# Edge groups of 512 instead of 1024, their keys spread by TensorE, in a graph network's count tables

## The chip, the cores and the metric

The kernel is one program on one core of a Trainium2 chip. The metric is the device time of one execution in microseconds (us).

## The reference

There are four layers on 3125 nodes with 256 features and 53,125 edges, sorted by their target. Each one adds to x what it makes of a layer-normalized x: three graph convolutions (a mean over each node's neighbours, two weight matrices, batch norm), slice attention, a hypergraph convolution, and a mixture of eight experts. For the change only the first graph step counts:

```python
agg = segment_sum(h[src], dst, num_segments=N)
deg = segment_sum(ones, dst, num_segments=N)
out = (agg / maximum(deg, 1)) @ Wl + bl + h @ Wr
```

All graph layers use the same edges.

## The kernel before

**Tables.** The kernel turns the edge list into a dense table of counts in DRAM, edges from node to node, in 16-bit floats. The table has five blocks (NB = 5) of 640 target nodes (BC), and a block has 128 x 16000 counts, 4.1 MB. Aggregation is then a matmul of the node features with the table's chunks. There are two tables, `at_counts` and `odd_counts`, so that scatters into the one can run while those into the other land. Later DVE adds each odd chunk to the even one (`sum_tables`, L1210), ACT writes the sum back (L780), and PE aggregates (L1860 for the degrees, L1868 for the features, L1886 for the products with the weights). The last block is done in two halves (L1221, L1922, L1931, L1950).

**Clearing.** ACT issues DMAs that write zeros into the tables (L704, one per table and block) from `zeros16`, which lies in a buffer that the first layer's output overwrites later. The first two are issued at the start. Then ACT issues nine small loads of vectors (L712) and two of weights (L713, L714), and then, for b = 1 to 4, waits until both tables' block b-1 is cleared and issues both clears of block b. Only after this loop come ACT's square root for the layer norm (`ln_sqrt(1)`, L722) and the copies for the first layer, which wait until everything is cleared.

**Keys.** Each edge has a key, its address in the table. The keys stand as `ekeyT` (104 rows of 512, one row per partition) and as `ekey` (416 columns of 128, made by PE's transposes). Scatters add, but a key that stands twice in one scatter, or in two scatters in flight, would be lost. So DVE compares each column of 128 with all the keys of its group: `edges_of`, one SCALAR_TENSOR_TENSOR with an accumulator per column (L1104), and three small operations per group (L1109 to L1111). They give one of the equal edges the count, and send the others to spare cells. A group is GQ = 8 columns, 1024 edges; there are NG = 52 groups. Its keys must be on all 128 partitions: SP stores `ekeyT` to DRAM (`key_rows`, L434) and loads each group back, broadcast, into one of LOOK = 4 buffers (L437, L443).

**Scatters.** POOL issues one indirect DMA per column (L598), eight for an even group into `at_counts`, eight for the next into `odd_counts`. Before each group it waits for the group's indices (`idx_ready`) and for all scatters of the group before the last, which went to the same table. Before the first group it waits until the blocks that the first eight groups touch are cleared, and before the ninth until all are.

**Order on DVE.** Each engine runs its program in order. DVE compares two turns of LOOK groups (8 groups); then it takes the layer norm's statistics of x, waits for ACT's square root, works out the release counts (`block_releases`), and goes into a loop of five, each with the normalized rows of five tiles, one turn of groups, and the low halves of those rows. The rest of the turns follow, and then the sums of the tables.

**Order on SP.** It starts loading table chunks only when all groups are compared, since chunks and `ekey` share the buffer `ring`. It loads a block when POOL's scatters of that block have landed (`released`).

```python
            ln_sqrt(1)
            wait(w0_in, 16 * 11)
            wait(zeroed, 2 * 16 * (NB + 1))
```

Of the kernel before, what the change touches and what calls it, by code (L numbers as in the profile page):

```python
# [4 lines left out]
P = 128  # L5
# [7 lines left out]
NB = T // BT  # L13
# [6 lines left out]
EC = -(-EDGES // P)  # L20
GQ = 8
GE = GQ * P
NG = EC // GQ
RW = 512
ER = EC * P // RW
RQ = RW // P
LOOK = 4
FIRST_GROUPS = 8
GROUP = GQ * 16
AROW = T * BC  # L30
# [66 lines left out]
def build(nc, x, src, dst, w, out):  # L97
    ctx = ExitStack()
    with ctx:
# [19 lines left out]
        ad = ad_flat.rearrange("(b p r) a -> p b (r a)", b=NB, p=P)  # L119
        key_rows = dram("key_rows", (EC * P,), fp32)  # L120
        xn_rows = dram("xn_rows", (T * P, F), fp32)
# [4 lines left out]
        ring = sb("ring", [P, 8192])  # L126
# [35 lines left out]
        def halves(d):  # L162
# [21 lines left out]
        release = harena[0:1, 11320:11320 + 4 * NR].bitcast(i32).rearrange("p (a b) -> p a b", a=4)  # L184
        row_block, first_block = harena[0:ER, 11313:11314], harena[0:1, 11314:11315]
        ekey = ring[:, 0:EC]
        espare = ring[:, EC:2 * EC]
        eweight = ring[:, 832:832 + 2 * GE - P]
        weight_ps = ps[:, 4:8, :].rearrange("p k c -> p (k c)")[:, 0:2 * GE - P]
        krow = ring[:, 2752:2752 + LOOK * GE].rearrange("p (a c) -> p a c", a=LOOK)  # L190
        ejunk = [late[:, q * GE // 2:(q + 1) * GE // 2].bitcast(fp16) for q in range(6)] + [
            ring[:, 6848 + q * GE // 2:6848 + (q + 1) * GE // 2].bitcast(fp16) for q in range(GQ - 6)]
        ecount = ring[:, 7872:7872 + 4 * GQ].rearrange("p (a c) -> p a c", a=4)
# [49 lines left out]
        for k in range(2):  # L243
# [63 lines left out]

        consts_ready, filled, edges_in, x_in, zero_ready, zeroed = map(sem, (
            "consts_ready", "filled", "edges_in", "x_in", "zero_ready", "zeroed"))
        fold_in, fold_pe, fold_dve = map(sem, ("fold_in", "fold_pe", "fold_dve"))  # L310
        keys_dve, key_stored = map(sem, ("keys_dve", "key_stored"))
        piece_in = [sem(f"keys_or_last_piece_in{s}") for s in range(LOOK)]
        compared, idx_ready, even_added, odd_added, tables_summed = map(sem, ("compared", "idx_ready", "even_groups_added", "odd_groups_added", "tables_summed"))
# [49 lines left out]
        def last_in(q):  # L363
            if q < LOOK:
                return piece_in[q], 16 * (NG // LOOK + 1)
            return odd_in[0], 16 * (-(-(NB * NB) // 2) + 1)
# [54 lines left out]
        def _(sp):  # L421
# [10 lines left out]
            sp.dma_start(bsl_row, w["L0_ffn_b_slice"].rearrange("(a g) -> a g", a=1)).then_inc(fold_in, 16)  # L432
            sp.wait_ge(keys_dve, 1)
            sp.dma_start(key_rows.rearrange("(p c) -> p c", c=RW), ekeyT).then_inc(key_stored, 16)  # L434
            sp.wait_ge(key_stored, 16)
            for s in range(LOOK):
                sp.dma_start(krow[:, s, :], key_rows[s * GE:(s + 1) * GE].partition_broadcast(P)).then_inc(piece_in[s], 16)  # L437
            sp.dma_start(xrows[:, 0:T - 1, :], x[0:(T - 1) * P, :].rearrange("(t p) d -> p t d", p=P)).then_inc(x_in, 16)
            sp.dma_start(xrows[0:TAIL, T - 1, :], x[(T - 1) * P:N, :]).then_inc(x_in, 16)
            with sp.Fori(0, NG // LOOK - 1) as i:  # L440
                for s in range(LOOK):
                    sp.wait_ge(compared, LOOK * i + (s + 1))
                    sp.dma_start(krow[:, s, :], key_rows[bass.ds(i * (LOOK * GE) + (s + LOOK) * GE, GE)].partition_broadcast(P)).then_inc(piece_in[s], 16)  # L443
            sp.wait_ge(idx_ready, NG)
# [115 lines left out]
        def _(pool):  # L560
# [31 lines left out]
            def add_group(g, table, added):  # L592
# [4 lines left out]
                for c in range(g * GQ, (g + 1) * GQ):  # L597
                    nc.gpsimd.indirect_dma_start(  # L598
                        out=table, out_offset=bass.IndirectOffsetOnAxis(ap=eidx[:, c:c + 1], axis=0),
                        in_=evalue[:, c:c + 1], in_offset=None, compute_op=ALU.add).then_inc(added, 16)  # L600

            pool.wait_ge(idx_ready, 1)
            cleared = pool.value_load(release[:, 3, 0:1], min_val=64, max_val=64 + 32 * (NB - 1))
            pool.nop(nofuse=True)
            pool.wait_ge(zeroed, cleared)
            pool.nop(nofuse=True)
            for g in range(0, NG, 2):
                if g == FIRST_GROUPS:
                    pool.wait_ge(zeroed, 32 * (NB + 1))
                add_group(g, at_flat, even_added)  # L610
                add_group(g + 1, odd_flat, odd_added)

# [78 lines left out]
        def _(act):  # L691
            def wait(s, value):
                act.wait_ge(s, value)
                if not isinstance(value, int):
                    act.nop(nofuse=True)
# [6 lines left out]

            def clear(table, b):
                act.dma_start(table[:, b, :].rearrange("p (k c) -> p k c", c=ZW), zeros16[:, 0:ZW].unsqueeze(1).to_broadcast([P, AROW // ZW, ZW])).then_inc(zeroed, 16)  # L704

            for flat in (at_flat, odd_flat):
                act.dma_start(flat[ASIZE:ASIZE + GE * SPREAD, :].rearrange("(p n) a -> p (n a)", p=P), zeros16[:, 0:GE * SPREAD // P]).then_inc(zeroed, 16)
            clear(at, 0)
            clear(odd, 0)
            for l in range(3):  # L710
# [49 lines left out]
            wait(w0_in, 16 * 11)  # L760
            wait(zeroed, 2 * 16 * (NB + 1))
            wait(fold_dve, 6)
# [193 lines left out]
        def _(dve):  # L956
# [9 lines left out]
            def step(ins):  # L966

                o.mark(ins)
                o.settle()
# [7 lines left out]
            for k in range(2, NB):  # L977
# [8 lines left out]
            dve.wait_ge(fold_pe, 1)  # L986
            step(V.tensor_reduce(first_block, ps[0:1, 1, 0:2 * FIRST_GROUPS], AX.X, ALU.max))
            step(V.tensor_scalar(release[:, 3, 0:1], first_block, 32.0, 64.0, ALU.mult, ALU.add))
# [109 lines left out]
            def edges_of(i, ahead, groups=range(LOOK)):  # L1098

                for s in groups:  # L1100
                    dve.wait_ge(piece_in[s], i * 16 + (16 * ahead + 16))
                    g = i * (LOOK * GQ) + (ahead * LOOK + s) * GQ
                    for q in range(GQ):
                        ins = V.scalar_tensor_tensor(out=ejunk[q], in0=krow[:, s, :], scalar=ekey[:, bass.ds(g + q, 1)], in1=weight_ps[:, GE - P - q * P:2 * GE - P - q * P],  # L1104
                                                     op0=ALU.is_equal, op1=ALU.mult, accum_out=ecount[:, s, q:q + 1])
# [642 lines left out]
        def _(pe):  # L1748
# [87 lines left out]
            def nothing_between(q):  # L1836
                pass
# [455 lines left out]
```

## Time and profile before

| | us |
|---|---|
| median of 3 runs (2973.86 to 2995.41) | 2974.38 |
| the profiled execution | 2977.06 |
| its span | 2975.3 |
| busy PE, DVE, POOL | 2255.9, 1308.3, 889.9 |

The span is the time from the first to the last instruction in the trace, and what is left to the execution's own time lies around it. All row times count from the span's start.

### The profile page before, as it was taken

Reading aid. Unit: us, or ns where it says so; the run is one execution under the profiler, and the core shown is the slowest. Engines: PE = TensorE matmul, PEld = TensorE weight load, DVE = VectorE, ACT = ScalarE, POOL = GpSimd, SP = SyncE. Lnnn points to the kernel's source line nnn. Section 1 sums busy time; section 2 is a strip of 40 time slices with the busy share of each in tenths; the row PEclk is TensorE's granted clock in tenths of the full one; section 3 lists DMA queues with packets and bytes.
Section 4 is the critical chain, followed back from the end, with each engine's and each line's share of the span. In section 5 each row is a group of like instructions: output and inputs, shape, how many; then the busy total and the mean of one; then the engine's idle time right before and its main releaser. Section 6 shows DMA issues by size and latency. Waiting matters only on the chain.

```text
span 2975.3 us, 39530 instructions
## 1 busy us (share of the span) xinstructions
PE 2255.9 (76%) x14177; PEld 1771.6 (60%) x14177; DVE 1308.3 (44%) x2804; ACT 375.5 (13%) x789; POOL 889.9 (30%) x637
## 2 busy tenths in 40 slices
PE   1033200048989999999996878999999995899997
PEld 1022100035667776777773457888888884788886
DVE  7899999955341011111116855012311667111111
ACT  0011000000005000004102212001110000222222
POOL 4888888886830000000002410000000001333332
PEclk9976555569999999999997979999999986999999
DMA  9943333368770999960351000444344434567766
GB/s 346 329 80 50 44 48 50 50 215 282 188 227 0 234 194 261 248 184 0 100 188 50 0 1 1 144 144 132 123 142 143 143 104 130 163 190 210 211 194 176
DMA packets 298822, 425.26 MB, mean 143 GB/s; under 512 B 165858, under 2 KB 235513, under 8 KB 298655
## 3 DMA queue, kind: packets, MB, share of 16 engines
q1 hardware_dynamic: 116575, 295.72, 30.7%
q10 hardware_dynamic: 109760, 108.33, 13.3%
q0 software_dynamic: 72400, 20.04, 7.8%
q8 instruction: 55, 0.90, 0.1%
q14 instruction: 32, 0.26, 0.0%
HBM read 306.57 MB, written 100.17 MB: 137 GB/s over the span
## 4 chain that ended last, share of the span: by engine, by line
PE 64%; DVE 16%; issue 7%; DMA 4%; POOL 3%; ACT 2%; ACTq 2%; DVEq 1%; SPq 0%
PE ps L1868 16%; PE ps L2166 8%; PE ps L2167 8%; PE ps L2248 7%; PE ps L2239 7%; DVE late L1104 5%; PE ps L1800 4%; PE ps L1886 4%; DMA odd_counts<-tarena 3%; DVE ring L1104 3%; POOL at_counts L598 2%; PE ps L1999 2%; PE ps L2100 2%; PE ps L2123 2%; DMA xrows<-odd_counts 1%
## 5 line engine op out<-in xcount | busy, mean ns | idle before, releaser
L2166 PE MATMUL ps<-harena,ring 128*128 128x257 f16 x2500 | 558.1, 275 | 3.1 <-DVE harena L1521 1.4
L2167 PE MATMUL ps<-harena,ring 128*128 128x256 f16 x2500 | 557.7, 273 | 0.0
L1868 PE MATMUL ps<-ring,harena 128*128 128x320 f16 x3800 | 512.4, 297 | 1.4 <-ACT tarena L755 0.8
L1868 PEld LDWEIGHTS ps<-ring,harena 128*128 128x128 f16 x3800 | 371.8, 98 | 138.5 <-issue 3.1
L1104 DVE SCALAR_TENSOR_TENSOR late<-ring,ps 128x1024 f16<-128x1024 f32 x312 | 379.0, 1276 | 12.9 <-DMA ring<-key_rows 10.7
L598 POOL DMA_INDIRECT at_counts<-harena x208 | 330.2, 1588 | 111.7 <-issue 108.8
L598 POOL DMA_INDIRECT odd_counts<-harena x208 | 331.2, 1592 | 63.9 <-issue 63.0
L2166 PEld LDWEIGHTS ps<-harena,ring 128*128 128x128 f16 x2500 | 243.2, 97 | 42.1 <-DVE harena L1521 4.5
L2167 PEld LDWEIGHTS ps<-harena,ring 128*128 128x128 f16 x2500 | 243.4, 97 | 33.3
L652 POOL IOTA harena<- 1x32 int32 x1 | 0.2, 183 | 736.4 <-DVE xrows L1590 736.4
L1892 PE MATMUL ps<-ident,sc 128*1 128x128 f32 x4 | 1.0, 333 | 281.3 <-DVE sc L1050 281.3
L2248 PE MATMUL ps<-ring,harena 128*128 128x256 f32 x896 | 201.7, 382 | 10.4 <-ACT harena L948 8.9
L2239 PE MATMUL ps<-harena,ring 128*128 128x256 f32 (+1 forms) x1024 | 201.5, 355 | 1.2 <-DVE harena L1721 1.2
L2248 PEld LDWEIGHTS ps<-ring,harena 128*128 128x128 f32 x896 | 167.6, 190 | 39.2 <-issue 17.7
L2239 PEld LDWEIGHTS ps<-harena,ring 128*128 128x128 f32 x1024 | 177.0, 192 | 22.3 <-issue 1.6
L1185 DVE SCALAR_TENSOR_TENSOR feat<-ps,sc,late 128x640 f32<-128x640 f32 x30 | 26.5, 884 | 348.5 <-PE ps L1868 348.5
L623 POOL DMA_DIRECT2D wl<-L_ffn_W_out x1 | 0.7, 712 | 586.8 <-DVE feat L1185 586.8
L681 POOL DMA_INDIRECT x_sum<-harena x56 | 88.8, 1586 | 268.0 <-DVE harena L1731 237.3
L1892 PEld LDWEIGHTS ps<-ident,sc 128*1 128x1 f32 x4 | 0.2, 81 | 282.0 <-issue 282.0
L948 ACT ACTIVATE harena<-ps,harena 128x256 f32<-128x256 f32 (+1 forms) x256 | 114.4, 447 | 342.4 <-PE ps L2239 337.9
L1886 PE MATMUL ps<-feat,wl 128*128 128x320 f32 x448 | 125.5, 441 | 16.5 <-DVE feat L1185 15.5
L1800 PE MATMUL ps<-feat,wr 128*128 128x320 f32 (+1 forms) x480 | 130.1, 428 | 0.0
(395 smaller groups left out, 2556.0 us busy)
## 6 DMA issues: line engine op xcount, KB each, us to landing
ring<-at_counts SPq DMA_DIRECT2D x145, 800.0 KB, 4.4
ring<-L_ffn_W SPq DMA_DIRECT2D x64, 1024.0 KB, 5.6
ring<-ad_counts SPq DMA_DIRECT2D x50, 800.0 KB, 4.2
ring<-key_rows SPq DMA_DIRECT2D x52, 512.0 KB, 3.7
at_counts<-tarena ACTq DMA_DIRECT2D x5, 4000.0 KB, 15.3
odd_counts<-tarena ACTq DMA_DIRECT2D x5, 4000.0 KB, 27.7
at_counts<-ring ACTq DMA_DIRECT2D x25, 800.0 KB, 7.0
ad_counts<-xrows ACTq DMA_DIRECT2D x25, 800.0 KB, 7.6
```

Source lines behind the costliest of these rows:

```text
L598: nc.gpsimd.indirect_dma_start(out=table, out_offset=bass.IndirectOffsetOnAxis(ap=eidx[:, c:c + 1], axis=0), in_=evalue[:, c:c + 1], in_of ...
L681: nc.gpsimd.indirect_dma_start(out=x_sum, out_offset=bass.IndirectOffsetOnAxis(ap=to_row[:, j:j + 1], axis=0), in_=yrow[c % 2][:, i, :], i ...
L948: nc.scalar.activation(hT[s][:, k, 0:n], ps[:, k % 4, 0:n], ACT.Gelu, bias=evc[s][:, k:k + 1]).then_inc(e_gelu, 1)
L1104: ins = V.scalar_tensor_tensor(out=ejunk[q], in0=krow[:, s, :], scalar=ekey[:, bass.ds(g + q, 1)], in1=weight_ps[:, GE - P - q * P:2 * GE ...
L1800: ins = M(ps[:, 4 + n % 4, 0:c], weights[:, d, fo * P:(fo + 1) * P], feat[:, d, h * HB:h * HB + c], start=(d == 0), stop=(d == 3))
L1868: ins = M(ps[:, 2 * f + h, 0:c], part[:, t, (2 * k + f) * P:(2 * k + f + 1) * P], chunk[q][:, s, h * HB:h * HB + c], start=(t == 0 and par ...
L1886: ins = M(ps[:, k + h, 0:HB], wl2[:, d, fo * P:(fo + 1) * P], feat[:, d, h * HB:(h + 1) * HB], start=(d == 0), stop=(d == nfi - 1))
L1999: return M(ps[:, i % 4, 0:F], feat[:, d, i * P:(i + 1) * P], wl3[:, d, :], start=(d == 0), stop=(d == 3))
L2166: M(ps[:, i, 0:F + 1], lhs, hh[:, t, 0:F + 1], start=(t == 0), stop=False)
L2167: ins = M(ps[:, i, 0:F], lhs, hl[:, t, :], start=False, stop=(t == T - 1))
L2239: ins = M(ps[:, k % 4, 0:n * P], w1e[s][:, d, k * P:(k + 1) * P], xeT[s][:, d, 0:n * P], start=(d == 0), stop=(d == 1))
L2248: ins = M(ps[:, 4 + s, i * F:(i + 1) * F], hT[s][:, k, i * P:(i + 1) * P], w2e[s][:, k, :], start=(k == 0), stop=(k == EK - 1))
```

## The change

- A group is 4 columns, 512 edges, so that it is one row of `ekeyT`; there are 104 groups and 26 turns of four. The number of groups that DVE compares before the layer norm and in each round of its loop is still a turn of four (8 before, 4 in each round).
- The keys no longer go through DRAM. PE multiplies row g of `ekeyT` by a column of the identity spread over 128 columns (`spread_keys`); the result is in one of four PSUM banks, which DVE reads. The weights of the comparison stay in SBUF, and the copy of them to PSUM (L994) goes.
- The load of x waits until the odd table's first block is cleared.
- Each table has a semaphore of its own for the clears. ACT issues the clear of block b of a table when that table's block b-1 is cleared. The place of the loop on ACT is the same.
- POOL checks the clears before groups 0, 8 and 16 for the blocks that these and the groups before the next check touch, for the even table before the even group and for the odd one before the odd group, and before group 24 for all blocks.
- POOL's waits for the group before the last now stand after every four scatters, not eight.

```diff
-GQ = 8
+GQ = 4
+CHECKS = 3
-            sp.wait_ge(keys_dve, 1)
-            sp.dma_start(key_rows.rearrange("(p c) -> p c", c=RW), ekeyT).then_inc(key_stored, 16)
-            sp.wait_ge(key_stored, 16)
-            for s in range(LOOK):
-                sp.dma_start(krow[:, s, :], key_rows[s * GE:(s + 1) * GE].partition_broadcast(P)).then_inc(piece_in[s], 16)
+            sp.wait_ge(odd_zeroed, 32)
             sp.dma_start(xrows[:, 0:T - 1, :], ...)
-            with sp.Fori(0, NG // LOOK - 1) as i:
-                for s in range(LOOK):
-                    sp.wait_ge(compared, LOOK * i + (s + 1))
-                    sp.dma_start(krow[:, s, :], key_rows[...].partition_broadcast(P)).then_inc(piece_in[s], 16)
...
+            def blocks_cleared(k, table_zeroed):
+                if k < CHECKS:
+                    cleared = pool.value_load(release[:, 3, k:k + 1], min_val=32, max_val=32 + 16 * (NB - 1))
+                    pool.nop(nofuse=True)
+                    pool.wait_ge(table_zeroed, cleared)
+                    pool.nop(nofuse=True)
+                else:
+                    pool.wait_ge(table_zeroed, 16 * (NB + 1))
             for g in range(0, NG, 2):
-                if g == FIRST_GROUPS:
-                    pool.wait_ge(zeroed, 32 * (NB + 1))
+                check = g % FIRST_GROUPS == 0 and g <= CHECKS * FIRST_GROUPS
+                if check:
+                    blocks_cleared(g // FIRST_GROUPS, even_zeroed)
                 add_group(g, at_flat, even_added)
+                if check:
+                    blocks_cleared(g // FIRST_GROUPS, odd_zeroed)
                 add_group(g + 1, odd_flat, odd_added)
...
             for b in range(1, NB):
-                act.wait_ge(zeroed, 32 * (b + 1))
-                clear(at, b)
-                clear(odd, b)
+                act.wait_ge(even_zeroed, 16 * (b + 1))
+                clear(at, even_zeroed, b)
+                act.wait_ge(odd_zeroed, 16 * (b + 1))
+                clear(odd, odd_zeroed, b)
...
-            step(V.tensor_copy(weight_ps, eweight))
...
-                    dve.wait_ge(piece_in[s], i * 16 + (16 * ahead + 16))
+                    dve.wait_ge(keys_spread, i * LOOK + (ahead * LOOK + s + 1))
                     for q in range(GQ):
-                        ins = V.scalar_tensor_tensor(out=ejunk[q], in0=krow[:, s, :], scalar=ekey[:, bass.ds(g + q, 1)], in1=weight_ps[:, ...],
+                        ins = V.scalar_tensor_tensor(out=ejunk[q], in0=ps[:, LOOK + s, :], scalar=ekey[:, bass.ds(g + q, 1)], in1=eweight[:, ...],
...
+            def spread_keys(turn):
+                for g in range(turn * LOOK, (turn + 1) * LOOK):
+                    if turn > 0:
+                        pe.wait_ge(compared, g + 1 - LOOK)
+                    M(ps[:, LOOK + g % LOOK, :], ident[0:ER, g:g + 1].to_broadcast([ER, P]), ekeyT, start=True, stop=True).then_inc(keys_spread, 1)
+            spread_keys(0)
             (PE: transposes and products that fold the slice weights)
+            spread_keys(1)
             (PE: the two small products of the release counts)
-            with pe.Fori(0, NB) as b:
+            for b in range(NB):
+                spread_keys(b + 2)
                 pe.wait_ge(rows, b * BT + BT)
                 (PE: transposes and products(b) of the first layer)
+            for turn in range(NB + 2, NG // LOOK):
+                spread_keys(turn)
```

## Rows read from the trace of the kernel before

**Rows 1.** The page's 40 slices of 74.4 us: busy tenths of DVE and POOL.
```profile
DVE  7899999955341011111116855012311667111111
POOL 4888888886830000000002410000000001333332
```
**Rows 2.** The page's costliest groups: line, engine, operation, count, busy us, mean ns, idle before.
```profile
L1104 DVE SCALAR_TENSOR_TENSOR late<-ring,ps 128x1024 f16<-128x1024 f32 x312 | 379.0, 1276 | 12.9 <-DMA ring<-key_rows 10.7
L598 POOL DMA_INDIRECT at_counts<-harena x208 | 330.2, 1588 | 111.7 <-issue 108.8
L598 POOL DMA_INDIRECT odd_counts<-harena x208 | 331.2, 1592 | 63.9 <-issue 63.0
```
**Rows 3.** Timeline of POOL (start us, us): the first scatter and the last two.
```profile
43.27 1.74 POOL L598 DMA_INDIRECT at_counts<-harena  x1 [34.64 <-issue]
...
842.23 1.55 POOL L598 DMA_INDIRECT odd_counts<-harena  x1 [0.30 <-issue]
844.08 1.55 POOL L598 DMA_INDIRECT odd_counts<-harena  x1 [0.30 <-issue]
```
**Rows 4.** Timeline behind the last scatter: last odd loads, last half's products, batch norm's end.
```profile
847.22 5.50 SPq L495 DMA_DIRECT2D xrows<-odd_counts  x5
...
857.45 0.70 PE L1922 MATMUL ps<-ring,ones 128*128 128x245 f16 x5 [2.27 <-DVE ring L1221]
...
881.16 4.47 ACT L745 ACTIVATE feat<-tarena,bn_k 128x320 f32<-128x320 f32 x8 [0.83 <-DVE bn_k L1311]
```
**Rows 5.** Timeline of DVE: the weights' copy, the first group's first two comparisons and its last operation.
```profile
18.51 2.15 DVE L994 COPY ps<-ring 128x1920 f32<-128x1920 f32 x1
...
31.32 1.28 DVE L1104 SCALAR_TENSOR_TENSOR late<-ring,ps 128x1024 f16<-128x1024 f32 x1 [10.65 <-DMA ring<-key_rows]
...
32.52 1.28 DVE L1104 SCALAR_TENSOR_TENSOR late<-ring,ps 128x1024 f16<-128x1024 f32 x1
...
41.34 0.16 DVE L1111 TENSOR_TENSOR harena<-ring 128x8 int32<-128x8 f32 x1
```
**Rows 6.** Groups by line and form, 0 to 800 us: a comparison 512 wide; then the critical chain's 32 products.
```profile
L1081 DVE SCALAR_TENSOR_TENSOR late<-harena,ones 104x512 f16<-104x512 f32 x6 | 4.1, 691 | 0.2
...
904.79 8.62 PE ps L1800 x32
```
**Rows 7.** Timeline: ACT's clears of the second and last blocks, square root, and DVE behind it.
```profile
41.93 0.85 ACTq L704 DMA_DIRECT2D at_counts<-tarena  x1
...
133.68 0.70 ACTq L704 DMA_DIRECT2D odd_counts<-tarena  x1
134.41 1.28 ACT L722 ACT_TABLE_LOAD   x1 [134.41 <-issue]
...
135.97 0.32 DVE L1042 RECIPROCAL ln_r<-ln_s 128x25 f32<-128x25 f32 x1 [5.02 <-ACT ln_s L722]
...
144.90 1.72 DVE L1045 TENSOR_SCALAR feat<-xrows,ln_mv,ln_r 128x256 f32 x5 [0.64 <-DVE harena L1095]
```
**Rows 8.** L704 issued at 3 to 10 us, to landing; DMA queue (packets, MB, share) 78 to 105; windows.
```profile
DMA to landing us min/median/max: 15.3/21.5/27.7
...
q10 hardware_dynamic: 2080, 8.19, 79.8%
...
6.00:18.00 12.00, 1.10 (x5) 0.71 (x5) 8.71 (x15) 0.00 (x0) 2.56 (x5) 1.00 1.04 412
```
**Rows 9.** L598 to landing, issued at 80 to 100, 300 to 600 and 650 to 670 us.
```profile
DMA to landing us min/median/max: 6.0/9.3/10.1
...
DMA to landing us min/median/max: 2.9/3.0/5.0
...
DMA to landing us min/median/max: 13.2/16.7/20.9
```
**Rows 10.** Timeline of POOL at its one long stop.
```profile
675.91 1.55 POOL L598 DMA_INDIRECT at_counts<-harena  x1 [2.26 <-DMA at_counts<-harena]
689.75 1.55 POOL L598 DMA_INDIRECT at_counts<-harena  x1 [12.30 <-issue]
```

More of the change, by code:

```diff
@@ L119, in build @@
         ad = ad_flat.rearrange("(b p r) a -> p b (r a)", b=NB, p=P)
-        key_rows = dram("key_rows", (EC * P,), fp32)
         xn_rows = dram("xn_rows", (T * P, F), fp32)
@@ L184, in build @@
         release = harena[0:1, 11320:11320 + 4 * NR].bitcast(i32).rearrange("p (a b) -> p a b", a=4)
-        row_block, first_block = harena[0:ER, 11313:11314], harena[0:1, 11314:11315]
+        row_block, first_block = harena[0:ER, 11313:11314], harena[0:1, 11314:11314 + CHECKS]
         ekey = ring[:, 0:EC]
@@ L188, in build @@
         eweight = ring[:, 832:832 + 2 * GE - P]
[L189 to L192, printed above, removed]
+        ejunk = [late[:, q * GE // 2:(q + 1) * GE // 2].bitcast(fp16) for q in range(GQ)]
         ecount = ring[:, 7872:7872 + 4 * GQ].rearrange("p (a c) -> p a c", a=4)
@@ L305, in build @@
         past_single = late[0:1, 2620:2620 + SINGLES * EXPERTS].rearrange("p (c e) -> p c e", c=SINGLES)
-        consts_ready, filled, edges_in, x_in, zero_ready, zeroed = map(sem, (
-            "consts_ready", "filled", "edges_in", "x_in", "zero_ready", "zeroed"))
+        consts_ready, filled, edges_in, x_in, zero_ready, even_zeroed, odd_zeroed = map(sem, (
+            "consts_ready", "filled", "edges_in", "x_in", "zero_ready", "even_table_zeroed", "odd_table_zeroed"))
         fold_in, fold_pe, fold_dve = map(sem, ("fold_in", "fold_pe", "fold_dve"))
-        keys_dve, key_stored = map(sem, ("keys_dve", "key_stored"))
-        piece_in = [sem(f"keys_or_last_piece_in{s}") for s in range(LOOK)]
+        keys_dve, keys_spread = map(sem, ("keys_dve", "keys_spread"))
+        piece_in = [sem(f"last_piece_in{s}") for s in range(LOOK)]
         compared, idx_ready, even_added, odd_added, tables_summed = map(sem, ("compared", "idx_ready", "even_groups_added", "odd_groups_added", "tables_summed"))
@@ L364, in last_in @@
             if q < LOOK:
-                return piece_in[q], 16 * (NG // LOOK + 1)
+                return piece_in[q], 16
             return odd_in[0], 16 * (-(-(NB * NB) // 2) + 1)
@@ L432, in _ @@
             sp.dma_start(bsl_row, w["L0_ffn_b_slice"].rearrange("(a g) -> a g", a=1)).then_inc(fold_in, 16)
-            sp.wait_ge(keys_dve, 1)
-            sp.dma_start(key_rows.rearrange("(p c) -> p c", c=RW), ekeyT).then_inc(key_stored, 16)
-            sp.wait_ge(key_stored, 16)
-            for s in range(LOOK):
-                sp.dma_start(krow[:, s, :], key_rows[s * GE:(s + 1) * GE].partition_broadcast(P)).then_inc(piece_in[s], 16)
+            sp.wait_ge(odd_zeroed, 32)
             sp.dma_start(xrows[:, 0:T - 1, :], x[0:(T - 1) * P, :].rearrange("(t p) d -> p t d", p=P)).then_inc(x_in, 16)
             sp.dma_start(xrows[0:TAIL, T - 1, :], x[(T - 1) * P:N, :]).then_inc(x_in, 16)
-            with sp.Fori(0, NG // LOOK - 1) as i:
-                for s in range(LOOK):
-                    sp.wait_ge(compared, LOOK * i + (s + 1))
-                    sp.dma_start(krow[:, s, :], key_rows[bass.ds(i * (LOOK * GE) + (s + LOOK) * GE, GE)].partition_broadcast(P)).then_inc(piece_in[s], 16)
             sp.wait_ge(idx_ready, NG)
@@ L600, in add_group @@
                         in_=evalue[:, c:c + 1], in_offset=None, compute_op=ALU.add).then_inc(added, 16)
+            def blocks_cleared(k, table_zeroed):
[6 more added lines that the diff above has]
+                    pool.wait_ge(table_zeroed, 16 * (NB + 1))
             pool.wait_ge(idx_ready, 1)
[L603 to L606, printed above, removed]
             for g in range(0, NG, 2):
-                if g == FIRST_GROUPS:
-                    pool.wait_ge(zeroed, 32 * (NB + 1))
+                check = g % FIRST_GROUPS == 0 and g <= CHECKS * FIRST_GROUPS
+                if check:
+                    blocks_cleared(g // FIRST_GROUPS, even_zeroed)
                 add_group(g, at_flat, even_added)
+                if check:
+                    blocks_cleared(g // FIRST_GROUPS, odd_zeroed)
                 add_group(g + 1, odd_flat, odd_added)
@@ L701, in _, with clear @@
             act.wait_ge(zero_ready, 1)
-            def clear(table, b):
+            def clear(table, zeroed, b):
                 act.dma_start(table[:, b, :].rearrange("p (k c) -> p k c", c=ZW), zeros16[:, 0:ZW].unsqueeze(1).to_broadcast([P, AROW // ZW, ZW])).then_inc(zeroed, 16)
-            for flat in (at_flat, odd_flat):
+            for flat, zeroed in ((at_flat, even_zeroed), (odd_flat, odd_zeroed)):
                 act.dma_start(flat[ASIZE:ASIZE + GE * SPREAD, :].rearrange("(p n) a -> p (n a)", p=P), zeros16[:, 0:GE * SPREAD // P]).then_inc(zeroed, 16)
-            clear(at, 0)
-            clear(odd, 0)
+            clear(at, even_zeroed, 0)
+            clear(odd, odd_zeroed, 0)
             for l in range(3):
@@ L760, in _ @@
             wait(w0_in, 16 * 11)
-            wait(zeroed, 2 * 16 * (NB + 1))
+            wait(even_zeroed, 16 * (NB + 1))
+            wait(odd_zeroed, 16 * (NB + 1))
             wait(fold_dve, 6)
@@ L986, in _ @@
             dve.wait_ge(fold_pe, 1)
-            step(V.tensor_reduce(first_block, ps[0:1, 1, 0:2 * FIRST_GROUPS], AX.X, ALU.max))
-            step(V.tensor_scalar(release[:, 3, 0:1], first_block, 32.0, 64.0, ALU.mult, ALU.add))
+            for k in range(CHECKS):
+                o.mark(V.tensor_reduce(first_block[:, k:k + 1], ps[0:1, 1, 0:FIRST_GROUPS * (k + 1)], AX.X, ALU.max))
+            o.settle()
+            step(V.tensor_scalar(release[:, 3, 0:CHECKS], first_block, 16.0, 32.0, ALU.mult, ALU.add))
             V.tensor_copy(ekey.rearrange("p (r a) -> p a r", a=RQ), ps[:, 0, 0:EC].rearrange("p (a r) -> p a r", a=RQ)).then_inc(keys_dve, 1)
@@ L992, in _ @@
                                    ekey.rearrange("p (g q) -> p g q", q=GQ), ALU.subtract))
-            step(V.tensor_copy(weight_ps, eweight))
+            o.settle()
             def fold_weights():
@@ L1100, in edges_of @@
                 for s in groups:
-                    dve.wait_ge(piece_in[s], i * 16 + (16 * ahead + 16))
+                    dve.wait_ge(keys_spread, i * LOOK + (ahead * LOOK + s + 1))
                     g = i * (LOOK * GQ) + (ahead * LOOK + s) * GQ
                     for q in range(GQ):
-                        ins = V.scalar_tensor_tensor(out=ejunk[q], in0=krow[:, s, :], scalar=ekey[:, bass.ds(g + q, 1)], in1=weight_ps[:, GE - P - q * P:2 * GE - P - q * P],
+                        ins = V.scalar_tensor_tensor(out=ejunk[q], in0=ps[:, LOOK + s, :], scalar=ekey[:, bass.ds(g + q, 1)], in1=eweight[:, GE - P - q * P:2 * GE - P - q * P],
                                                      op0=ALU.is_equal, op1=ALU.mult, accum_out=ecount[:, s, q:q + 1])
```

## The prediction

> **What bounds the kernel now.** I read the 40 slices first, to find the stretch that the change touches. The reader is to see two engines filled at once up to about 600 us: DVE at nine tenths, and POOL at eight tenths, and POOL goes on after DVE has dropped [rows 1]. So the comparisons, although they are the larger sum, need not be the bound. The costliest groups say what POOL's eight tenths are: 416 scatters of 1.59 us [rows 2], and the POOL timeline shows that they start 1.857 us apart (842.23 to 844.08), with 0.30 us of "issue" between them, which is no wait for anyone. POOL is full at eight tenths. From the first scatter at 43.27 to the end of the last at 845.63 are 802.4 us [rows 3]; 416 x 1.857 = 772.5 of them are the bare rate, and 29.9 are losses.
>
> Next comes the end of the stage. SP issues the last odd chunks 1.6 us after the last scatter, PE takes up the last half at 857.45, and the batch norm's result is used at 881.16 [rows 4]: 35.5 us behind POOL's end. PE was busy with the half before until then and so waited for little. Both chains, POOL's scatters and PE's blocks after 627, end together here. DVE's earlier finish frees PE's blocks to start earlier, but the last half block can't be loaded before POOL's last scatter. **The end of the stage is POOL's end plus the tail**, and everything later in the kernel hangs on it unchanged. The question is when POOL ends.
>
> **What is saved at the start.** The first group's comparison waited 10.65 us for the keys from DRAM and began at 31.32; its indices were there at 41.5, and POOL began 1.8 us later [rows 3, 5]. The copy at 18.51 goes, and PE has the first row spread by then: 32 products of 320 columns take 8.62 us, 0.27 each, so one of 512 columns takes 0.43 [rows 6]. It is bounded by 0.43 and twice that, if TensorE ran at half its clock there; either is under a group's time on DVE, so I cost it at nothing. A comparison 1024 wide comes every 1.20 us (31.32 to 32.52) and lasts 1.276; one 512 wide lasts 0.691 [rows 5, 6]. That gives 1.20 - 0.585 = 0.62 at the low end and 0.69 at the high end; I take 0.67, and with 0.7 us for the small operations 3.4 us per group. Reading keys from PSUM and weights from SBUF, where it was the other way round, I cost at nothing (bounds -0.05 and +0.1 us each; DVE has slack for either). So the first indices are there at 18.9 + 3.4 = 22.3 and POOL starts at 24, 19 us earlier. The clears allow it: the even table's first block landed at 2.95 + 15.3 = 18.3 and the odd one's at 3.75 + 27.7 = 31.5 [rows 8], less perhaps 2 us without the key loads beside it, and POOL's second group comes at 32.
>
> **What is lost behind it.** DVE's program still has eight groups before the layer norm, but they are now half as large: 32 scatters instead of 64. Eight groups feed POOL for 8 x 7.43 = 59.4 us; with 2 us for the second group and the folding of the slice weights between DVE's groups, they end at about 85. DVE has compared them by about 57 and finished its statistics by 70. Then it waits for ACT's square root, and ACT gets to this only after its last clear. Before, that was seen as 5.02 us of idle DVE: the last clear is issued at 133.68, the square root follows, DVE goes on at 135.97 [rows 7]. POOL didn't feel it, as it had 64 scatters in hand until 43.27 + 119 = 162. Now it will.
>
> When does ACT get there? The last clear needs the odd table's fourth block landed: three pairs of blocks after the second block's clear, which was issued at 41.93 [rows 7]. A pair is 8.19 MB and took 79.8% of 27 us, 21.5 us of all DMA engines; the rest went to keys and scatters [rows 8]. The key loads go and the scatters, while they run, add about 12%. Three pairs from 40 us, with 2 us for the rest of x, are 40 + 2 + 24 + 24 + 22 = 112. The ends: 118 if the stretch keeps more of its 27 us, 106 if scatters cost the clears nothing. The separate semaphores save the gap between pairs, which is in these figures. From the last clear to DVE are 2.3 us, from there to the normalized rows 8.9, and 1.8 for them [rows 7]; with a group of 3.4 the ninth indices come at 128.4, and POOL starts again at 128.8 after **some 43 us of idleness**. From the second check on, at 189 us, all clears are done; the checks cost nothing.
>
> Behind this DVE keeps ahead: a round of its loop is four groups (14 us) plus 4 us of rows, and PE's share of a round, with four spreads, stays under the 29.7 us that POOL needs for four groups. All is compared at about 500 instead of 626 us.
>
> **Losses on the way.** Before they were 29.9 us. Of these 416 x (1.590 - 1.552) = 16 are longer issues [rows 2, 3], 1.552 being the plain issue, and 14 the one stop at 673 to 690 [rows 10]. The first part stays. The second belongs to the stretch in which two blocks of chunks are loaded, summed and stored back to back; this moves to about 500 us and stays. Here lies the new wait. A group's first scatter now needs the landing of a scatter issued 5 x 1.857 = 9.3 us earlier, where it was 16.7. In the quiet stretch a scatter lands in 3.0 us, in the clearing in 9.3, in the loaded stretch in 16.7 [rows 9]. With landing L a pair of groups takes 5.6 + L instead of 14.9 us: 22.3 in the loaded stretch. Over 60 us this costs 60 x (1 - 14.9 / 20.4) = 16 with a mean of 14.8 between 13 and 16.7. I take it in place of the 14, since fewer scatters in flight are also fewer to stop for, plus 3 us for the later blocks: 35 in all.
>
> **The sum.** POOL ends at 128.8 + 384 x 1.857 (713) + 35 = 877, 31 us later than before. The tail is shorter: PE is idle by then and waits for the chunks, so it can start 6 to 7 us behind POOL's end instead of 11.8 (1.6 to the issue as before, some 4 to the first chunk and 1 for its sum). PE has been idle before and may start slower; between 0 and -5 I take -3. +28 us on the profiled execution's 2977.06 is 3005; it stands 2.7 us above the median of the runs, so the forecast is **3002**, 0.9% above.
>
> **The rivals.**
>
> *The waits of every four scatters cost more than the stop they replace (slower).* The point is a landing of 9.3 us. If the 12 us gap [rows 10] stays on top of the waits, and the three later blocks, of 24 us of loads each, also see 14 us landings where they were paced by PE before, the losses are 16 + 12 + 16 + 3 x 24 x (1 - 14.9 / 19.6) = 61 in place of 35: 3028. For it: 16.7 in the loaded stretch. Against: fewer in flight, and a slower POOL loads the queue less. Half of it gives 3015.
>
> *The clears run faster.* In the first stretch the DMA engines moved 412 GB/s [rows 8], when little but clears was in them. At this a pair takes 19.9 us, the last clear is issued at 42 + 60 = 102, and POOL resumes 10 to 12 us earlier: 2991. Against it: at 78 to 105 the engines were as busy and a pair still took 21.5 us of them.
>
> The Trainium skill (DMA: Bandwidth & Descriptors, Where 436 GB/s comes from) gives the path through SBUF's ports 436 GB/s; by this a pair would take 18.8 us and the kernel, by an estimate from that page, 2988. The same page's Specifications give the memory 358 GB/s per core; by this a pair would be 22.9 us and the kernel 3001, the scatters' share left out in both. The trace's 21.5 us lies between the two.
>
> *POOL is never short.* If DVE's wait for ACT did not bite, POOL would run from 24 to 24 + 2 + 772 + 35 = 833, 13 us earlier than before: 2959. For it the saved start; against it the order of the programs, which the change leaves as it was. To be free of it ACT would have to be through by 70 us, with 33 MB of clears to land before.
>
> *The spreads hold DVE up.* PE takes them between the first layer's products. If a round of the loop took over 29.7 us, POOL would wait in five rounds, 5 us each: 3027. PE's work per round speaks against.
>
> **How the numbers follow.** The forecast's case gets 0.50, with a range of its own of 2990 to 3014; 0.28 of it lies within 1% and 0.22 above. About 1% is what a measurement of this kernel can tell from no change; it is 3004. The waits get 0.17 (slower), the faster clears 0.17 (within 1%), POOL never short 0.08 (within), the spreads 0.05 (slower), and 0.03 is for a gain of over 1% that I have no mechanism for. So faster 0.03, within 1% 0.53, slower 0.44. The range 2980 to 3024 leaves out the fed POOL, the spreads and the upper part of the waits.
>
> **What would show it.** POOL's first scatter at about 24 us; a gap in POOL from about 85 to 129 that ends with a DVE operation; ACT's square root at 112 to 115; comparisons of about 0.7 us, over by 500; the last scatter at 870 to 885. Waits of POOL for its own DMAs only in the clearing and at 500 to 600. The forecast is wrong if the gap is missing or under 30 us, if the losses after 129 are not 25 to 45, or if the batch norm's end does not follow POOL's by 30 to 35 us.

## The result and the profile after

The changed kernel takes 2998.8 us, median of 20 runs (2991.4 to 3021.3), against 2973.8 before (20 runs, 2971.6 to 2995.4). The ratio is 1.0081, 95% interval 1.0066 to 1.0097. Forecast were 3002 and a range of 2980 to 3024.

The profiled execution of the changed kernel took 3021.26 us, 22 more than the median; where these 22 us lie is told below. Up to the end of the first layer it agrees with a second profile, so its rows are used for that stretch. First the page's slices (75.5 us each) and its costliest groups, which answer to [rows 1] and [rows 2].

```profile
DVE  6498886501321011111115864212221677211111
POOL 6388887788840000000001420000000000333332
...
L587 POOL DMA_INDIRECT at_counts<-harena x208 | 328.0, 1577 | 125.9 <-issue 78.3
L587 POOL DMA_INDIRECT odd_counts<-harena x208 | 332.7, 1599 | 78.4 <-issue 61.9
L1105 DVE SCALAR_TENSOR_TENSOR late<-ps,ring 128x512 f16<-128x512 f32 x416 | 287.3, 746 | 16.9 <-issue 8.6
L1771 PE MATMUL ps<-harena,ident 104*128 104x512 f32 x208 | 187.3, 1018 | 123.2 <-DVE late L1105 122.1
```

The comparisons fell from 1276 to 746 ns each, their busy time from 508 us (the 379.0 of [rows 2] and 128.8 of the same line's other form, 104 writing to ring) to 287.3, both 416 in number. POOL's row is busy earlier, has a dent in the second slice, and ends a little later. The timeline of the first 140 us shows the dent, with what ended it.

```profile
24.23 1.75 POOL L587 DMA_INDIRECT at_counts<-harena  x1 [17.38 <-issue]
...
76.96 0.20 DVE L1024 TENSOR_TENSOR ln_mv<-ln_st 128x25 f32<-128x25 f32 x1
...
109.54 0.54 ACTq L702 DMA_DIRECT2D odd_counts<-tarena  x1
110.12 1.28 ACT L721 ACT_TABLE_LOAD   x1 [110.12 <-DMA odd_counts<-tarena]
...
111.67 0.32 DVE L1043 RECIPROCAL ln_r<-ln_s 128x25 f32<-128x25 f32 x1 [33.54 <-ACT ln_s L721]
...
120.36 1.71 DVE L1046 TENSOR_SCALAR feat<-xrows,ln_mv,ln_r 128x256 f32 x5 [0.65 <-DVE harena L1096]
...
125.83 1.55 POOL L587 DMA_INDIRECT at_counts<-harena  x1 [41.06 <-DVE harena L1112]
```

Read it backwards. POOL stands 41.06 us and is released by the last operation of a group's comparison on DVE. DVE stood 33.54 us before that and was released by ACT's square root. ACT began it 0.04 us after its last clear had been issued, at 109.54; a clear waits for the same table's block before to land, so at bottom the 33.54 us are a wait for clears to land. The first scatter is 19 us earlier than in [rows 3], and DVE's resumption 24 us earlier than in [rows 7]; but the eight groups that POOL had in hand were over at 84.8.

The end of the stage answers to [rows 4]: the last scatter, the last odd loads, PE's last half, and the use of the batch norm.

```profile
870.24 1.55 POOL L587 DMA_INDIRECT odd_counts<-harena  x1 [0.30 <-issue]
...
875.77 3.46 SPq L484 DMA_DIRECT2D xrows<-odd_counts  x5
...
880.63 1.21 PE L1935 MATMUL ps<-ring,ones 128*128 128x245 f16 x5 [37.23 <-DVE ring L1222]
...
904.19 4.47 ACT L744 ACTIVATE feat<-tarena,bn_k 128x320 f32<-128x320 f32 x8 [0.84 <-DVE bn_k L1312]
```

PE waited 37.23 us for the last half, where it had waited 2.27 before: PE's own blocks no longer take part, and POOL alone sets the end. The batch norm's result is used at 904.2 in place of 881.2, 23.0 us later, and the median is 25.0 us later.

### The profile page after: what moved, and what is told of

Same layout as the page of the kernel before. It is cut to its first block, busy times and chain, and to the rows that moved or that the text cites. A ratio compares the mean times of both kernels' runs of the same rounds, so it can differ in the third digit from the quotient of the medians.

```text
span 3019.5 us, 40231 instructions
## 1 busy us (share of the span) xinstructions
PE 2430.4 (80%) x14385; PEld 1814.2 (60%) x14385; DVE 1115.1 (37%) x2961; ACT 375.6 (12%) x789; POOL 887.5 (29%) x637
## 4 chain that ended last, share of the span: by engine, by line
PE 47%; POOL 18%; ACTq 14%; issue 7%; DVE 6%; DMA 5%; ACT 2%; DVEq 0%; POOLq 0%; SPq 0%
ACTq L800 12%; POOL odd_counts L587 9%; POOL at_counts L587 8%; PE ps L2179 8%; PE ps L2180 8%; PE ps L2261 7%; PE ps L2252 7%; PE ps L1881 4%; PE ps L1809 4%; DMA odd_counts<-tarena 3%; PE ps L2113 2%; PE ps L2012 2%; PE ps L2136 1%; DMA odd_counts<-harena 1%; PE ps L2053 1%
## 5 line engine op out<-in xcount | busy, mean ns | idle before, releaser
L1105 DVE SCALAR_TENSOR_TENSOR late<-ps,ring 128x512 f16<-128x512 f32 x416 | 287.3, 746 | 16.9 <-issue 8.6
L1771 PE MATMUL ps<-harena,ident 104*128 104x512 f32 x208 | 187.3, 1018 | 123.2 <-DVE late L1105 122.1
L1771 PEld LDWEIGHTS ps<-harena,ident 104*128 104x128 f32 x208 | 50.4, 287 | 253.9 <-DVE late L1105 237.7
L1899 PEld LDWEIGHTS ps<-feat,wl 128*128 128x128 f32 x448 | 87.0, 196 | 161.6 <-issue 123.6
## 6 DMA issues: line engine op xcount, KB each, us to landing
at_counts<-tarena ACTq DMA_DIRECT2D x5, 4000.0 KB, 20.9
```

The source lines that it names most:

```text
L1105: ins = V.scalar_tensor_tensor(out=ejunk[q], in0=ps[:, LOOK + s, :], scalar=ekey[:, bass.ds(g + q, 1)], in1=eweight[:, GE - P - q * P:2 * ...
L1771: M(ps[:, LOOK + g % LOOK, :], ident[0:ER, g:g + 1].to_broadcast([ER, P]), ekeyT, start=True, stop=True).then_inc(keys_spread, 1)
L1899: ins = M(ps[:, k + h, 0:HB], wl2[:, d, fo * P:(fo + 1) * P], feat[:, d, h * HB:(h + 1) * HB], start=(d == 0), stop=(d == nfi - 1))
```

## The experiments

Each was timed beside the kernel before on the same chip. "POOL over" is the end of the last scatter, "norm" the first use of the first layer's batch norm, both in the profiled execution.

| kernel | median us | ratio (95%) | first scatter | gap for DVE | POOL over | norm |
|---|---|---|---|---|---|---|
| before | 2973.8 | | 43.3 | none | 845.6 | 881.2 |
| changed | 2998.8 | 1.0081 (1.0066 to 1.0097) | 24.2 | 41 | 871.8 | 904.2 |
| changed, again | 2997.3, one run | | 24.3 | 41 | 870.0 | 902.3 |
| four turns first | 2958.5 | 0.9946 (0.9929 to 0.9962) | 23.9 | none | 832.7 | 865.9 |
| root after third clears | 2992.8 | 1.0062 (1.0046 to 1.0079) | 24.0 | 8.5 + 28.5 | 866.4 | 898.4 |
| before, one turn first | 3008.9 | 1.0117 (1.0100 to 1.0134) | 42.8 | 46 | 883.7 | 915.8 |
| groups of 1024, spread | 2965.6 | 0.9972 (0.9960 to 0.9983) | 31.7 | none | 836.5 | 870.8 |
| clears in pairs | 3004.5 | 1.0101 (1.0084 to 1.0118) | 24.3 | 46.5 | 876.1 | 909.2 |
| three turns first | 2969.0 | 0.9987 (0.9972 to 1.0002) | 23.9 | 13 | 842.0 | 874.7 |
| five turns first | 2959.2 | 0.9942 (0.9922 to 0.9961) | 24.3 | 0.8 | 830.5 | 863.7 |
| four turns, spreads doubled | 2958.8 | 0.9944 (0.9926 to 0.9962) | 25.3 | none | 831.8 | 864.9 |

**The changed kernel again.**

> The changed kernel as it is, profiled a second time. The profiled execution on record took 3021 us, where the median of its runs is 2999; in its trace the batch norm of the first layer is over 23 us later than before, and another 21 us come between there and 1390 us, in ACT's transposing loads of the table. If these 21 us belong to that one execution, this one takes 2992 to 3001 and its first layer's batch norm ends at about 904 us, with the transposes over by about 1310. If they belong to the change, it takes over 3010 again.

It took 2997.26 us; POOL's gap was 40.8 us and the norm was used at 902.3. So the 22 us above the median in the first profile are that execution's own. The waits of that execution name the place: ACT's root for the second layer's batch norm waits for table transposes (L800) that ACT has to issue first.

```profile
ACT bn_k L725 <- DMA xrows<-at_counts: 265.1, 1, 265.1
```

The last transpose is issued at 1385.8 in the first profile and at 1330.8 in this one (1284.9 before; about 1310 was expected). The root itself comes at 1389.1 in the first and at 1365.5 in this one, where it waits for DVE, as before the change. Why the transposes were slower in one execution was not tried.

**Four turns of groups before the layer norm.** PE's spreads are moved the same way, so that each engine's order still fits.

```diff
             edges_of(0, 1)
+            edges_of(0, 2)
+            edges_of(0, 3)
             dve.wait_ge(x_in, 32)
...
-                edges_of(i, 1)
+                edges_of(i, 3)
...
-            with o.loop_from(NB + 2, NG // LOOK, 2 * LOOK) as i:
+            with o.loop_from(NB + 4, NG // LOOK, 2 * LOOK) as i:
...
             spread_keys(1)
+            spread_keys(2)
+            spread_keys(3)
...
-                spread_keys(b + 2)
+                spread_keys(b + 4)
```

> The changed kernel with four turns of groups (16 groups, 64 scatters, as many as before the change) compared before the layer norm in place of two. Theory (POOL runs dry while DVE waits for ACT's square root): the idle 41 us at 85 to 126 go, POOL ends near 832 in place of 874, the kernel takes 2955 to 2965. Rival (the waits after every four scatters and the stops in the loaded stretch carry the loss): POOL still ends within 15 us of 874, the kernel takes 2985 to 3000. Rival (PE's blocks become the bound once POOL is early): the gain stops at 10 to 20 us, 2980 to 2990.

2958.5 us, as the theory had it: 40 us less than the changed kernel, 15 less than before. On this kernel's timeline of POOL and DVE, the wait for ACT is still there (18.23 us), and POOL works through it:

```profile
110.65 0.54 ACTq L702 DMA_DIRECT2D odd_counts<-tarena  x1
...
112.77 0.32 DVE L1043 RECIPROCAL ln_r<-ln_s 128x25 f32<-128x25 f32 x1 [18.23 <-ACT ln_s L721]
...
139.17 1.56 POOL L587 DMA_INDIRECT odd_counts<-harena  x1 [0.30 <-issue]
141.04 1.68 POOL L587 DMA_INDIRECT odd_counts<-harena  x1 [0.30 <-issue]
143.03 1.55 POOL L587 DMA_INDIRECT odd_counts<-harena  x1 [0.30 <-issue]
```

The two rivals fall: POOL was over 39 us earlier, so its other waits do not carry the loss, and the gain did not stop at PE.

**The square root after the clears of block 2.**

```diff
             for b in range(1, NB):
                 ...
                 clear(odd, odd_zeroed, b)
+                if b == 2:
+                    act.wait_ge(ln_var, 1)
+                    nc.scalar.activation(ln_s[:, :], ln_r[:, :], ACT.Sqrt).then_inc(ln_std, 1)
...
-            ln_sqrt(1)
```

> The changed kernel with ACT's square root for the first layer norm issued after the clears of block 2 (at about 90 us) in place of after those of block 4 (at 110); DVE's order stays. Theory: DVE goes on 20 us earlier, POOL's gap falls from 41 to about 21 us and the kernel from 2999 to about 2979. Rival (the gap is not what costs the time): no change, 2995 to 3002.

The expectation missed: only 6 us came back, not 20. DVE went on at 79 us, and POOL's first gap shrank to 8.5 us, but a second one of 28.5 opened behind the next four groups. The timeline of this kernel shows a second lock behind the first:

```profile
78.98 0.23 ACT L720 ACTIVATE ln_s<-ln_r 128x25 f32<-128x25 f32 x1 [9.87 <-DVE ln_r L1033]
...
131.82 1.64 ACT L770 ACTIVATE harena<-feat 128x256 f32 x5 [52.62 <-DMA odd_counts<-tarena]
132.42 1.77 DVE L1141 SCALAR_TENSOR_TENSOR harena<-feat,harena 128x256 f32 x5 [28.54 <-ACT harena L770]
...
134.70 11.74 PE L1800 MATMUL ps<-feat,wr 128*128 128x320 f32 x32 [39.90 <-ACT feat L773]
...
147.48 0.75 DVE L1107 SCALAR_TENSOR_TENSOR late<-ps,ring 128x512 f16<-128x512 f32 x1 [11.17 <-PE ps L1773]
```

In DVE's loop the low halves of the rows wait for ACT's high halves, and ACT waits for all clears to land before it makes them. Then the next spreads stand on PE behind the first layer's products, 11.17 us more. So DVE delivers four groups and compares no more until 147. In the changed kernel DVE compares its second round from 144.5, so the earlier square root brings the groups behind the first four no sooner. What decides is how many scatters POOL has in hand until the clears are through, not the square root.

**The kernel before, with one turn first**, so with 32 scatters in hand and nothing else of the change.

```diff
-            edges_of(0, 1)
             dve.wait_ge(x_in, 32)
...
-                edges_of(i, 1)
+                edges_of(i, 0)
...
-            with o.loop_from(NB + 2, NG // LOOK, 2 * LOOK) as i:
+            with o.loop_from(NB + 1, NG // LOOK, 2 * LOOK) as i:
```

> The kernel before the change, with one turn of its groups (4 groups of 1024, 32 scatters, as many as in the changed kernel) compared before the layer norm in place of two; keys through DRAM, groups of 1024, waits after every eight scatters, the clears as they were. Theory: POOL is dry from 103 us until DVE, held by ACT to 136, delivers the fifth group at about 157; a gap of 54 us, of which nearly all reaches the end, so 3015 to 3030. Rival (the loss of the changed kernel comes from its waits, its spreads or its clears, none of which is in here): within 5 us of 2974.

3008.9 us, 35 over before, from a gap of 46.20 us. The direction is the theory's and the rival's 2974 is far off, but the range of 3015 to 3030 was missed by 6 us, since a gap of 54 had been expected (ACT's root came at 127 in place of 136).

```profile
100.78 1.55 POOL L598 DMA_INDIRECT odd_counts<-harena  x1 [0.31 <-issue]
148.53 1.55 POOL L598 DMA_INDIRECT at_counts<-harena  x1 [46.20 <-DVE harena L1111]
```

The loss is to be had without a single spread, short group or new semaphore. POOL is over 38 us later and the kernel 35 us: the amount of work before the layer norm is enough to explain it.

**Groups of 1024 with keys spread by TensorE.**

```diff
-GQ = 4
+GQ = 8
...
+        spread_ps = [ps[:, LOOK + 2 * k:LOOK + 2 * k + 2, :].rearrange("p k c -> p (k c)") for k in range(2)]
...
-in0=ps[:, LOOK + s, :]
+in0=spread_ps[s % 2]
...
-                    if turn > 0:
-                        pe.wait_ge(compared, g + 1 - LOOK)
-                    M(ps[:, LOOK + g % LOOK, :], ident[0:ER, g:g + 1]..., ekeyT, ...).then_inc(keys_spread, 1)
+                    if g >= 2:
+                        pe.wait_ge(compared, g - 1)
+                    for h in range(2):
+                        ins = M(ps[:, LOOK + 2 * (g % 2) + h, :], ident[0:ER, 2 * g + h:2 * g + h + 1]..., ekeyT, ...)
+                    ins.then_inc(keys_spread, 1)
```

> The changed kernel with its groups set back to 1024 edges (8 columns, waits after every eight scatters, eight groups or 64 scatters before the layer norm); the keys still come from TensorE, two PSUM banks per group and two groups ahead, and the clears stay with a semaphore per table. Theory (the loss is the smaller amount of work in hand, not the spreading and not the clears): first scatter at about 30 us, no gap of over 5 us before 500 us, POOL over at 825 to 838, 2952 to 2963. Rival (the spreading by TensorE costs time of its own, by PE's order or by DVE reading PSUM): over 2970. For the waits after every four scatters: if they cost more than those after every eight, POOL's idle time in the loaded stretch is below the 16 us of the run with four turns first.

2965.6 us, 3 above the range, with POOL over at 836.5 as expected. Here DVE's comparisons last until 615 us, and PE's blocks are the later chain, as they were before: PE comes to the last half at 847.0 after a wait of 2.27 us only, 10.5 us behind POOL's end (8.8 in the changed kernel, after a wait of 37). The norm is used 34.3 us behind POOL's end in place of 32 to 33, so that chain costs some 2 us. This kernel is 8 us faster than before, so spreading and clears together gain by themselves, and what lost the time in the change is the shorter group with the count of turns left as it was.

It also bears on the question of the waits. POOL's timeline has the same stop as in [rows 10], in the stretch in which the first two blocks are loaded:

```profile
665.83 1.55 POOL L589 DMA_INDIRECT at_counts<-harena  x1 [2.79 <-DMA at_counts<-harena]
679.07 1.55 POOL L589 DMA_INDIRECT at_counts<-harena  x1 [11.68 <-issue]
```

With waits after every four scatters no profile has the 12 us stop; there are short waits for POOL's own scatters. These are the changed kernel's:

```profile
515.38 1.56 POOL L587 DMA_INDIRECT at_counts<-harena  x1 [1.01 <-DMA at_counts<-harena]
...
528.94 1.55 POOL L587 DMA_INDIRECT odd_counts<-harena  x1 [6.33 <-DMA odd_counts<-harena]
...
541.00 1.55 POOL L587 DMA_INDIRECT at_counts<-harena  x1 [2.77 <-DMA at_counts<-harena]
...
553.24 1.55 POOL L587 DMA_INDIRECT odd_counts<-harena  x1 [4.91 <-DMA odd_counts<-harena]
...
758.60 1.55 POOL L587 DMA_INDIRECT odd_counts<-harena  x1 [4.70 <-DMA odd_counts<-harena]
```

They are 15.0 us in the loaded stretch and 4.7 later, 19.7 in all; in the eight profiles with waits after every four scatters they sum to 16 to 20 us. Against that stand 14.5 us with groups of 1024 and 14.6 before. But the kernel before with one turn first also waits after every eight scatters, and has no stop:

```profile
704.57 1.55 POOL L598 DMA_INDIRECT odd_counts<-harena  x1 [2.02 <-DMA odd_counts<-harena]
...
724.94 1.55 POOL L598 DMA_INDIRECT at_counts<-harena  x1 [4.27 <-DMA at_counts<-harena]
```

It loses 6.3 us. So the waits after every four scatters cost 2 to 14 us more than those after every eight, and that they take the place of the stop is not shown.

**The clears in pairs again.**

```diff
             for b in range(1, NB):
                 act.wait_ge(even_zeroed, 16 * (b + 1))
-                clear(at, even_zeroed, b)
                 act.wait_ge(odd_zeroed, 16 * (b + 1))
+                clear(at, even_zeroed, b)
                 clear(odd, odd_zeroed, b)
```

> The changed kernel with ACT's clears in pairs again: both clears of a block are issued when both of the block before have landed; POOL's checks and all else stay. Theory (POOL's gap ends when ACT is through with its clears): the last clear is issued some 4 to 10 us later than at 109.5, POOL's gap grows from 41 to 45 to 51 us, and the kernel takes 3002 to 3009. Rival (the separate semaphores did nothing for the time): 2995 to 3001.

The last clear was issued at 114.8 in place of 109.5, POOL's gap grew by 5.5 us, and the kernel takes 3004.5, 5.7 more. So a microsecond of the clears was a microsecond of the kernel while POOL was dry; the separate semaphores gave back 5 to 6 us of what the short groups took.

**Three turns first.** The edit is that of four turns with one turn less.

> The changed kernel with three turns of groups (12 groups, 48 scatters) before the layer norm. Theory: each group in hand covers 7.4 us of the 41; four more leave a gap of about 11 us, POOL ends near 844, the kernel takes 2966 to 2973, between 2999 with two turns and 2958.5 with four. Rival (a threshold other than the scatters in hand, as an order of PE and DVE that four turns happened to fix): like one of the two.

2969.0 us, as fast as the kernel before within the noise, with a gap of 13.1 us. While POOL is dry, the scatters in hand decide in proportion: 32 give 2998.8, 48 give 2969.0, and the 16 between them take POOL 29.7 us; 64 give 2958.5, where the gap is shut.

**Five turns first**, likewise with one turn more.

> The changed kernel with five turns of groups (20 groups, 80 scatters) before the layer norm. Theory: four turns already cover DVE's wait (POOL had no gap in that run), so a fifth brings nothing: 2956 to 2962, as with four. Rival (the gain with four turns came from a better order of DVE's work in general, more of which is better still): under 2954.

2959.2 us: nothing more to gain, once the gap is shut.

**Four turns first, each spread twice.**

```diff
+                    M(ps[:, LOOK + g % LOOK, :], ident[0:ER, g:g + 1].to_broadcast([ER, P]), ekeyT, start=True, stop=True)
                     M(ps[:, LOOK + g % LOOK, :], ident[0:ER, g:g + 1].to_broadcast([ER, P]), ekeyT, start=True, stop=True).then_inc(keys_spread, 1)
```

> The kernel with four turns first, and each spreading product issued twice, the second over the first, 208 products in place of 104; outputs are the same. Theory (the spreads lie beside POOL's work and cost nothing): 2955 to 2963, no gap in POOL. Rival (the spreads hold DVE up between the first layer's products, and through it POOL): over 2965, with gaps of POOL at 140 to 230 us that end on DVE.

2958.8 us. At the start the second spreads cost 1.3 us at the first scatter and 3.4 at the third group (43.56 in place of 40.20). POOL's last scatter still ends 1 us earlier, since its longer issues sum to 12 us in this profile and to 16 in the one with four turns; a cost of a few us does not show beside that. And the test is weaker than it looks: with twice the products the mean granted clock was 0.79 in place of 0.50 between 300 and 480 us, and at the upper level both spreads of a group together (2.1 us) took no longer than one alone in the kernel with four turns (2.08, at 0.50). These are the two spreads of one group (granted 1.00 from 402 to 412 us) and of another (0.50 from 413 to 420):

```profile
403.29 1.12 PE L1773 MATMUL ps<-harena,ident 104*128 104x512 f32 x2 [2.09 <-DVE late L1105]
404.25 1.02 PE L1774 MATMUL ps<-harena,ident 104*128 104x512 f32 x2
...
414.08 2.07 PE L1773 MATMUL ps<-harena,ident 104*128 104x512 f32 x2 [1.48 <-DVE late L1105]
415.95 1.91 PE L1774 MATMUL ps<-harena,ident 104*128 104x512 f32 x2
```

The better sign that the spreads are hidden is that POOL has no gap behind DVE after 44 us.

## Why the prediction was right

**What bounds.** That POOL's scatters set the end of the stage held in the changed kernel and in all those made from it but the one with groups of 1024: in each PE stands idle for 36 to 37 us before the last half. With groups of 1024, and before, PE's blocks end last by some 2 to 3 us; in the kernel before with one turn first both chains end together (PE waited 2.47 us). The norm follows POOL's end by 32.0 to 33.3 us wherever POOL bounds, by 34.3 with groups of 1024 and by 35.5 in [rows 4]: the -3 us of the tail. Inside the tail the working was less good: PE took up the last half 8.8 us behind POOL's end, not 6 to 7, because SP issued the last odd loads 4.0 us behind it and not 1.6; from there to the norm it was 23.6 us (23.7 before), so the 2 us that had been kept for a slower PE were not needed. The two errors cancel. Behind the first layer the median moved 2 us more than the norm did, which was not looked into.

**The start.** First scatter at 24.23 (24 forecast). A comparison comes every 0.67 us and a group takes 3.15 us in the first turns and 3.6 in the loop (3.4 forecast). POOL waited 1.5 us (2 forecast), but before the third group, for DVE, which folded the slice weights between the second and the third; before the second, whose clear was the reason given, it did not wait. The size was right there by luck.

**The gap.** Forecast from 85 to 128.8, 43 us; it ran from 84.8 to 125.8, 41.06 us. Of the difference 2.5 us are the clears: the last was issued at 109.54 instead of 112. ACT had its second block's clear out at 32.1 already and not at 40, but the first of the three pairs had landed only at 67.7 (66 forecast), beside the load of x issued at 29; the other two took 21.5 and 20.3 us instead of 24 and 22. From the last clear to POOL's restart were 16.3 us, 16.8 forecast. DVE's statistics ended at 78.1 and not by 70, since DVE waited 8.7 us for x; the wait for ACT covered this. The check before the ninth group stands at this restart and not at 189 us, as the forecast had it; it held nothing up, though the last clear landed only at about 130. The Trainium skill (DMA: Bandwidth & Descriptors, Specifications) has a memory limit of about 358 GB/s per core and a fabric ceiling of 435; the stretch from 84 to 125 us moved 402 GB/s, so this trace's clears ran above the one and below the other.

**The losses.** 35 us were forecast after the restart; POOL ended at 871.8, and 871.8 - 125.8 - 713 is 33. Longer issues were 14 of this (16 forecast), its waits for its own scatters 20 (19 forecast). The size was right; the reason, that fewer scatters in flight take the stop away, is not shown, since the stop was also missing in one kernel with 16 in flight.

**Terms that were off.** The spreads were costed at 0.43 to 0.86 us each, from the count of 32 in [rows 6]. The trace counts an fp32 product as two instructions: 104 spreads stand as 208, of 1.02 us each, so a spread takes 2.0 us, over twice the forecast's upper bound. It was hidden all the same: a group takes 3.6 us on DVE and 7.4 on POOL. And the chain of waits was told only half: the square root is the first of two locks. That the forecast came out right with it alone is in part luck: in the changed kernel the second lock opens (ACT's copies begin at 130.2) before DVE comes to it at 136.3. The edit at the square root, planned from that half, missed by 14 us.

**The rivals.** The clears were faster than forecast by 2.5 us, not by 10. The waits every four scatters cost 2 to 14 us more than those every eight, not 26. The spreads did hold DVE up (4.2 us at 144.5), but no gap of POOL behind 126 ends on DVE. POOL never short was the right price for the wrong kernel: 2959 was forecast for it, and with four turns first it is 2958.5.

## What to carry to other kernels

A loop count that says how many pieces of work stand before a wait is a quantity of time; when the piece is halved, that cover is halved, and an engine two places down the line runs dry. So when the size of a piece is changed, look for every place that counts pieces, and for each find the wait that they covered: here two more turns of groups before the wait turned 1.0081 into 0.9946. To find how much cover is needed, follow the wait to its last cause; moving the first lock (the square root) out of the way only showed the second.

## What the runs showed of the hardware

- POOL issued an indirect scatter of 128 values every 1.857 us, 1.55 of it busy, with either group size and also just after a wait. Longer issues (up to 3.2 us) add 12 to 18 us in all, and all but 2 us of this at most fall behind the start of DVE's 16-bit sums of tables. That the sums cause them was not tried.
- With up to 16 scatters in flight while table chunks are loaded (landings of 13.2 to 20.9 us, [rows 9]), POOL stopped once for 12 us between two scatters of one group, where the program has no wait, in two of three profiles: 12.30 us before and 11.68 with groups of 1024, but not in the kernel before with one turn first. With at most eight in flight it did not, in any of eight profiles. What the stop is was not tried.
- An fp32 product of 512 columns over 104 rows, which the trace counts as two instructions, took 2.1 us while the granted clock was 0.50, the lower level of TensorE's clock (1.2 GHz), and 1.0 to 1.1 us at the upper (2.4 GHz; 1.00 between 46 and 53 us in the kernel with the spreads doubled). The four of the changed kernel's first turn took 5.61 us, 1.4 each, though the granted clock shown there is 1.00.
